# Attention rounds on TensorE: gates, projections and layer products ahead of the turns of the probabilities

## The reference

```python
x = x + _L0_attn_ref(_layernorm(x), ...)      # cumulative-sum "attention", rank 64
x = x + _L0_xattn_ref(_layernorm(x), ctx_1024, ...)
x = x + _L0_ffn_ref(_layernorm(x), ...)       # FP4 quantised gate, up and down
# the middle part:
normed = _rmsnorm(hidden_states, norm_w)
v_pool = jnp.concatenate([normed, memory_state], axis=1)
logits = jnp.einsum('bsd,btd->bst', q, k) * scale        # causal, plus 77 context keys
attn = jax.nn.softmax(logits, axis=-1)
h_tilde = jnp.einsum('bst,bth->bsh', attn, v_pool)
alpha = jax.nn.sigmoid(jnp.einsum('bsh,oh->bso', hidden_states, gate_w) + gate_b)
return (1.0 - alpha) * hidden_states + alpha * h_tilde
```

## Time and profile before

| | us |
|---|---|
| median of 3 runs (lowest, highest) | 555.36 (553.91, 555.95) |
| the profiled execution, its own time | 555.8 |
| its span, first to last instruction | 553.7 |
| PE busy in the span | 526.2 (95%) |
| DVE, POOL, ACT busy | 452.8, 408.1, 341.2 |

### The profile page before, as it was taken

One profiled execution on the slowest core, in us unless ns is written; L12 is line 12 of the kernel. 1 busy time (PEld: TensorE's weight loads), 2 busy tenths in 40 slices (PEclk: granted clock), 3 DMA queues, 4 the chain that ended last, 5 costly groups with the idle time before them and its releaser, 6 DMA issues.

```text
span 553.7 us, 10914 instructions
## 1 busy us (share of the span) xinstructions
PE 526.2 (95%) x3091; PEld 457.6 (83%) x3091; DVE 452.8 (82%) x1144; ACT 341.2 (62%) x807; POOL 408.1 (74%) x637
## 2 busy tenths in 40 slices
PE   7988998989989989999999998999999999999997
PEld 4866787878878778878888887899899999999996
DVE  3697589785798866887679867999899999999886
ACT  4342743736645348354486557787777788878763
POOL 4164958948649488399596947788988888888864
PEclk9998999999999999999999999999999999999999
DMA  8720500000000000000000000000000000000001
GB/s 228 208 77 2 156 2 0 2 2 0 1 0 1 1 0 1 1 2 2 0 2 1 1 2 0 1 20 19 20 20 19 19 19 19 19 19 19 25 24 49
DMA packets 16129, 13.85 MB, mean 25 GB/s; under 512 B 3883, under 2 KB 15839, under 8 KB 16095
## 3 DMA queue, kind: packets, MB, share of 16 engines
q1 hardware_dynamic: 16095, 13.43, 8.0%
HBM read 9.23 MB, written 4.19 MB: 24 GB/s over the span
## 4 chain that ended last, share of the span: by engine, by line
PE 73%; DVE 11%; issue 8%; ACT 5%; POOL 1%; DVEq 1%; ACTq 0%; POOLq 0%
PE ps L1017 17%; PE ps L1018 16%; PE ps L1019 16%; PE ps L1216 8%; PE ps L1390 3%; PE ps L1204 2%; PE ps L1214 2%; PE ps L1107 1%; ACT xn_sums L707 1%; PE ps L1135 1%; DVE X L1540 1%; PE ps L1264 1%; DVE st L1471 1%; DVE nT_l L1480 1%; DVE gz L1557 1%
## 5 line engine op out<-in xcount | busy, mean ns | idle before, releaser
L1017 PE MATMUL ps<-keys_h,nT_h 128*128 128x256 f32 (+6 forms) x272 | 85.7, 315 | 1.9 <-DVE keys_l L1480 1.4
L1018 PE MATMUL ps<-keys_l,nT_h 128*128 128x256 f32 (+6 forms) x272 | 83.3, 306 | 0.0
L1019 PE MATMUL ps<-keys_h,nT_l 128*128 128x256 f32 (+6 forms) x272 | 82.9, 305 | 0.0
L1017 PE MATMUL ps<-parts,xq_parts 128*128 128x512 f32 (+1 forms) x192 | 75.3, 392 | 0.0
L1018 PE MATMUL ps<-parts,xq_parts 128*128 128x512 f32 (+1 forms) x192 | 72.2, 376 | 0.0
L1019 PE MATMUL ps<-parts,xq_parts 128*128 128x512 f32 (+1 forms) x192 | 72.0, 375 | 0.0
L1216 PE MATMUL ps<-V,probT 128*128 128x256 f32 x288 | 67.4, 379 | 0.0
L750 ACT ACTIVATE prob<-ps,nbias 128x205 f32<-128x205 f32 (+7 forms) x32 | 25.7, 803 | 63.3 <-DVE nbias L1563 63.2
L1216 PEld LDWEIGHTS ps<-V,probT 128*128 128x128 f32 x288 | 54.5, 189 | 7.7
L1017 PEld LDWEIGHTS ps<-keys_h,nT_h 128*128 128x128 f32 x272 | 51.2, 188 | 6.2 <-DVE keys_l L1480 1.8
L627 POOL TENSOR_TENSOR probT<-prob,probT 128x704 f32<-128x704 f32 x31 | 47.6, 1535 | 9.3 <-ACT probT L824 9.3
(11 more groups left out here) (237 smaller groups left out, 1592.2 us busy)
## 6 DMA issues: line engine op xcount, KB each, us to landing
X<-in_x_dram SPq DMA_DIRECT2D x8, 512.0 KB, 5.0
out_dram<-X SPq DMA_DIRECT2D x32, 128.0 KB, 1.7
early<-in_L_ffn_w_down_dram SPq DMA_DIRECT2D x1, 704.0 KB, 6.9
early<-in_L_ffn_w_gate_dram SPq DMA_DIRECT2D x1, 640.0 KB, 4.5
early<-in_L_ffn_w_up_dram SPq DMA_DIRECT2D x1, 640.0 KB, 5.9
ctx_rows<-in_ctx_dram SPq DMA_DIRECT2D x1, 308.0 KB
early<-in_L_attn_Winv_dram SPq DMA_DIRECT2D x1, 256.0 KB, 3.8
early<-in_L_attn_WQ_dram SPq DMA_DIRECT2D x1, 256.0 KB, 5.1
```

The costliest lines, as they stand in the source:

```text
L1017: mm(o, wh, mh, start=start, stop=False, **kw)
L1018: mm(o, wh, ml, start=False, stop=False, **kw)
L1019: return mm(o, wl, mh, start=False, stop=stop, **kw)
```

## The change

Only PE's `batch` is edited; no instruction is added or taken away on any engine. In rounds 4, 6 and 7 the turns of tile i-1 come behind the gates and projections of the same round and not in front of them. Rounds 0 to 3, 5 and 8 keep their order. In round 6 the gates come first, then the projections t = 0, 1, then the turns. In the last batch only the gates of rounds 4 and 6 change places with the turns.

```diff
                     if i < TPB:
                         logits_tile(b, i)
+                    if more and i == 4:
+                        proj_tiles(b * 2 + 2, (2, 3))
                     if more and i == 5:
                         y_half(b + 1, 0)
+                    if more and i == 7:
+                        proj_tiles(b * 2 + 3, (2, 3))
+                    if i in (4, 6):
+                        for t in GATES[i]:
+                            gate_tile(b, t)
+                    if more and i == 6:
+                        proj_tiles(b * 2 + 3, (0, 1))
...
                     elif 1 <= i <= TPB:
                         turn_tile(b, i - 1)
                     if more:
-                        if i == 4:
-                            proj_tiles(b * 2 + 2, (2, 3))
-                        if i == 7:
-                            proj_tiles(b * 2 + 3, (2, 3))
...
-                    for t in GATES[i]:
-                        gate_tile(b, t)
+                    if i in (0, 1):
+                        for t in GATES[i]:
+                            gate_tile(b, t)
                     if i == 1:
                         keys_products(b, 1)
-                    if more and i == 6:
-                        proj_tiles(b * 2 + 3, (0, 1))
```

## The result

The changed kernel takes 552.15 us, median of 8 runs (550.93 to 553.65), beside 555.56 (553.63 to 557.25, 8 runs) for the kernel before: ratio 0.9941, interval 0.9918 to 0.9964. That is 3.4 us, twice the forecast 1.5. One run of the kernel before (1347.79 us) and one of `front_4_7_again` (654.88 us), both in the last comparison, were disturbed: the medians count them, the ratios do not. The spans of the two profiled executions are 553.7 and 550.7 us. In the changed kernel DVE's lines are numbered four higher.

The account below looks back on a forecast made before the run. PE, 95% busy, was taken as the bound, its idle time mostly waits behind DVE's scans. Gains of 0.5, 0.5, 0.45 and 0.06 summed to 1.5 us, from 555.36 to 553.8; own range 552.9 to 554.7, whole range 552.3 to 555.9.

Parts of the forecast that it names:

- Round 4: Projection ahead of tile 3's turns: DVE's scan and `turn_xn` in round 5 come 0.51 us earlier in three batches.
- surcharge behind the mask product: Round 4's first projection product straight behind the mask product: taken as 0.05 us extra, bounds 0 and 0.19.
- most of it given back: Round 6: PE stands 0.46 us for `xnT_low`, turns follow; of 0.51 us it keeps 0.08 in batches 0 and 1.
- slower, through round 6: Rival, chance 0.08: round 4's shift is lost before `xnT_low`, PE loses 0.43 us a batch; 556.7 us, at dearest 557.9.
- a second gain, capped: Round 7: scan 0.92 us earlier, but POOL's L505 holds L1527; keys product gains 0.5 us in batches 0 and 1.
- the second case: Rival, chance 0.20: POOL does not hold DVE back; signs were L1527 at 0.69 and keys wait about 0.9 us.
- Batch 2: No idle time at its keys product: 0.34 us from round 6, 0.03 in round 7, perhaps 0.08: 0.45 us.
- The sum: Whole kernel: 0.5 + 0.5 + 0.45 + 0.06 = 1.5 us gained, giving 553.8 us.
- The port does not bite: Rival, chance 0.20: DVE slips between POOL instructions in round 7; batches 0 and 1 win 0.92 us each; 553.0 us.
- No gain: Rival, chance 0.14: something else ties down DVE's run and each shift ends in another wait; 555.3 us.
- both slower cases: Rivals: round 6's turns behind PE's wait, 556.7 us, chance 0.08; ACT late in round 4, 559.3 us, chance 0.03.
- ACT's cover in round 4: Later `probT` copies on ACT fit in its 4.17 us wait for `gz`, leaving 0.9 us; cost nothing.

Follow-up runs that it names:

- front_4_7_again: Repeat of rounds 4 and 7 in the new order, round 6 in the old, against the kernel before: 551.17 us, ratio 0.9934.
- front_4_again: Repeat of only round 4 in the new order, against the kernel before: 554.13 us, 226.32 us from tile 0 to the gates of b3.
- front_7_again: Repeat of only round 7 in the new order, against the kernel before: 552.63 us (10 runs), ratio 0.9956.
- front_6: Only round 6 in the new order, against the kernel before: 555.02 us in one run.
- front_4_7: Rounds 4 and 7 in the new order, round 6 in the old, against the kernel before: 551.25 us (6 runs), ratio 0.9918.
- front_4: Only round 4 in the new order, against the kernel before: 555.17 us in one run, with a stretch at 1.2 GHz.
- pool_short: The changed kernel without POOL's multiplication of the rounded weights back by their scale, ahead of L505: 552.07 us in one run.
- second comparison: The changed kernel, unedited, timed once more beside the kernel before: 553.07 us (10 runs) beside 554.95, ratio 0.9967.
- front_7: Only round 7 in the new order, against the kernel before: 550.91 us in one run, tile 0 at 47.90.

## Why the prediction was wrong

The measured 552.15 lies below the range 552.3 to 555.9. Two things made the 1.5 us of the sum into 3.4: the gain of round 7 was taken too small, and the range had no room for how much the first stage differs between executions. The mechanism of the change itself was mostly as described. By part of a pass, shifts of the repeated changed kernel against the repeated kernel before:

| from, to | forecast | measured | front_4_again | front_7_again | front_6 | front_4_7 |
|---|---|---|---|---|---|---|
| tile 0, turn_xn b0 | -0.51 | -0.51 | -0.48 | +0.03 | +0.03 | -0.51 |
| turn_xn b0, keys b0 | +0.02 | -0.19 | 0.00 | -0.87 | +0.47 | -0.88 |
| keys b0, turn_xn b1 | -0.51 | -0.54 | -0.51 | -0.01 | +0.01 | -0.49 |
| turn_xn b1, keys b1 | +0.02 | -0.21 | -0.01 | -0.83 | +0.28 | -0.88 |
| keys b1, turn_xn b2 | -0.51 | -0.50 | -0.46 | +0.06 | 0.00 | -0.45 |
| turn_xn b2, gates b3 | +0.06 | -0.08 | -0.03 | -0.43 | -0.11 | -0.49 |
| sum | -1.43 | -2.03 | -1.49 | -2.05 | +0.68 | -3.70 |

(The forecast column is the prediction's 0.5, 0.5 and 0.45 for the batches less the 0.51 already gained; batch 3 is left out.)

- **Round 4.** Right: 0.51 forecast, 0.50 to 0.54 measured in each batch, and front_4 shows that it is this round alone. The surcharge behind the mask product was taken too low, 0.31 - 0.23 = 0.08 and not 0.05.
- **Round 6.** The wait of 0.46 in batch 0 came as forecast (0.44 by starts). PE was to keep 0.08 us over it and instead came 0.06 late. Unpriced were 0.11 us of the first product behind a wait and the turns themselves, 0.76 us where I had 0.70. What the prediction did not see at all is what this means as a choice: it called the round "most of it given back" and never asked what the kernel would do with round 6 left alone. front_4_7 against the changed kernel answers: 0.69 us between `turn_xn` and the keys product in batch 0, 0.67 in batch 1, 0.41 behind `turn_xn` in batch 2, less 0.10 in the rest, so 1.67 us are lost by that edit. The rival "slower, through round 6" had priced this: `front_6`, where round 4 brings nothing, is its condition, and the keys product of batch 0 comes 0.50 us late there against its 0.43.
- **Round 7, "a second gain, capped"; the step that failed.** The term was 0.49 us per batch at the first product of the ranks; it measured 0.69, and 0.68 to 0.70 at the keys product. The scan came 0.76 earlier and not 0.92, which lowers it. The collision with POOL was priced too dear: I charged the whole overlap of 0.43 us. Where the old L1527 starts inside an instruction of L505, the extra time is the overlap less about 0.14: before in b2, overlap 256.12 + 1.41 - 256.97 = 0.56, extra 1.10 - 0.69 = 0.41; changed in b0, 0.21 and 0.07; in b1, 0.18 and 0.04; in b2, 0.31 with the first of L505's two instructions (each is half of the 1.42) and 0.18. In the 15 such places of nine traces the difference is 0.11 to 0.15. The first of these stood in my own rows, 0.56 against 0.41, and is what I should have used: overlap 0.27 (with the scan 0.76 earlier), extra 0.12, and 0.64 instead of 0.49. The signs I gave pointed the same way: L1527 near 0.69 and a keys wait near 0.9 were to mean the second case, and they came at 0.76 and 0.95, though L1534 still stood beside L509 for 1.24. From there the shift reaches the keys product nearly whole; `pool_short` shows that only 0.2 us more was to be had there.
- **Batch 2.** Forecast 0.45 in all, measured 0.50 + 0.08 = 0.58.
- **The sum** for the passes should have been 2.0 us and was 1.5; 0.2 more lie behind them. That 2.2 us off the median of 555.36 is 553.2, close to the second comparison (553.07) and inside the range.
- **The rest, outside the change.** About 1.2 us of the first comparison's 3.4 are neither in the passes nor behind them. In its pair of traces tile 0 starts 1.00 us earlier: `y_half(0, 1)` begins 0.31 later, and from there tile 0 comes 1.31 sooner, with 3.4 and not 6.8 us at the lower clock. Fourteen profiled executions have tile 0 between 47.89 and 50.95 in no relation to the order of the passes, and passes and rest of one kernel repeat to 0.3 us, but for the stretch in front_4. The 8 runs of the changed kernel fell in two groups, four about 551.4 with a mean clock of 0.996 or 0.997 and four about 553.1 with 0.993; the ten of the second comparison are all in the upper one. The kernel before has such groups too: 16 of its runs have a mean clock of 1.000 and a median of 553.3, 46 have 0.993 to 0.997 and about 555.1. Lower group against lower and upper against upper, the change is worth 1.9 and 2.0 us, as the traces say, so the first comparison's 3.4 holds some luck in the draw. What 3.4 us at the lower clock cost is shown above; which executions get them, and why `y_half(0, 1)` starts 1.4 us apart, is not settled. My range gave the single profiled start no spread at all, and I had read the clock's row of the page without asking what that start would be another time.
- **Rivals.** "The port does not bite" is refuted by pool_short (1.24 to 0.68 us) although its time, 553.0, is what the second comparison shows: right in number by luck. "No gain" and both slower cases did not come as a whole: ACT's cover in round 4, in the changed kernel, shrank from 4.17 us to 0.74 (forecast 0.9) and held, by ACT's timeline of batch 0:

```profile
78.68 0.27 ACT L762 ACTIVATE probT<-ps 77x128 f32<-77x128 f32 x1 [2.80 <-PE ps L1204]
...
80.23 0.42 ACT L739 ACTIVATE th<-gz 128x256 f32<-128x256 f32 x1 [0.74 <-DVE gz L1561]
```

## What to carry to other kernels

Cost each moved place by itself, and then each combination with one place left out: here three places went together, two gained 3.7 us and the third took 1.7 of it back. A reordering pays where the moved work stood in front of what another engine waits for, and costs where it had filled a wait of PE's own, as the turns did in round 6. Count times from an anchor behind the first stage before two traces are compared; a difference that is there before the first edited instruction belongs to something else.

## What was not expected of the hardware

- DVE's products with two operands in SBUF and POOL's exclude each other by single instructions, in turn: beside L505 one DVE product took its free 0.69 us while POOL's pair stretched from 1.42 to 1.89, and the next DVE product took 1.10. The one that starts later loses the overlap less about 0.14 us (0.11 to 0.15 in 15 places of the old L1527).
- TensorE's first full-precision product of 512 columns behind a wait costs 0.34 us from start to start, behind the mask product 0.31, in the run 0.23.
- One kernel's first stage ends up to 2.1 us apart in different executions (front_7: 47.90 and 49.97). Of that, 1.7 us go with 3.4 us at 1.2 GHz behind a 1.88 us idle stretch of PE, and 0.4 with an earlier difference that no run explains. 1.7 us of filling products in that stretch kept the clock at 1.00 in both profiled executions that had it; of the twelve without it, two had 1.00 as well. Another stretch at the lower level, near 342 us, was there in some executions (0.89 from 335 to 350 us in the kernel before) and not in others (1.00 in its repetition), and the work behind the passes took 275.17 and 275.19 us: there it costs nothing.
